# Attention scores in a fused two-block transformer kernel: row halves of 64 instead of 128 contraction rows, issued in pairs

## The reference

```python
# block 0 (per sequence; H = 16 heads, D = 16)
h = _ln(x) * (1 + sc_msa) + sh_msa
qkv = h @ w_qkv + b_qkv                       # one window of 128: plain self attention
scores = einsum('qhd,khd->hqk', q, k) / sqrt(D)
o = einsum('hqk,khd->qhd', softmax(scores), v)
x = x + (o @ w_so + b_so) * g_msa
h = _ln(x) * (1 + sc_mca) + sh_mca            # cross attention to 128 context rows
scores = q k^T / sqrt(D);  keep the 16 largest of each row;  softmax over these
x = x + (o @ w_co + b_co) * g_mca
h = _ln(x) * (1 + sc_mlp) + sh_mlp            # SwiGLU, 1024 wide
x = x + (silu(a) * b @ w_m2 + b_m2) * g_mlp
# block 1: adaptive layer norms of x and the context, plain cross attention, x + (out @ Wp + bp)
```

## Time and profile before

| | us |
|---|---|
| time, median of 2 runs | 1040.71 (1040.1 to 1041.33) |
| span of the profiled execution | 1041.6 |
| PE, busy matmul time | 852.6 |
| DVE | 669.1 |
| ACT | 515.7 |
| POOL | 501.5 |
| mean granted TensorE clock | 0.947 of 2.4 GHz |

### The profile page before, as it was taken

The page is one execution under the profiler, slowest core; times in us unless marked ns, Lnnn a source line. Parts: engine busy times, 40 slices in busy tenths (PEclk is TensorE's granted clock), DMA queues, the critical chain, the costliest instruction groups (busy, mean ns, idle before and its releaser), DMA issues.

```text
span 1041.6 us, 21054 instructions
## 1 busy us (share of the span) xinstructions
PE 852.6 (82%) x5919; PEld 616.2 (59%) x5919; DVE 669.1 (64%) x2576; ACT 515.7 (50%) x2068; POOL 501.5 (48%) x576
## 2 busy tenths in 40 slices
PE   4879677888889966898898968778898996788897
PEld 4556356666556645676664645656665664566664
DVE  2247888844536888874445689885444679887443
ACT  0257334455557543345565744444455763334555
POOL 3246645633335555453433565554433555555334
PEclk9789899999999988999998998999999998899999
DMA  8441000000100100000000000000000000000000
GB/s 268 123 142 30 18 25 13 18 20 16 31 19 18 30 21 17 21 16 19 24 13 22 27 17 25 15 20 22 16 22 26 12 11 11 11 6 7 1 6 16
DMA packets 33860, 31.15 MB, mean 30 GB/s; under 512 B 7613, under 2 KB 29363, under 8 KB 33475
## 3 DMA queue, kind: packets, MB, share of 16 engines
q1 hardware_dynamic: 33731, 29.66, 9.8%
HBM read 21.20 MB, written 2.15 MB: 22 GB/s over the span
## 4 chain that ended last, share of the span: by engine, by line
PE 47%; DVE 32%; issue 9%; ACT 3%; POOL 3%; SPq 3%; DMA 2%; DVEq 1%; POOLq 0%; ACTq 0%
PE dense_bank L897 9%; PE score_bank L939 9%; PE o_bank L957 6%; DVE left L646 6%; DVE left L657 6%; PE dense_bank L904 6%; PE turn_bank L926 5%; DVE top L640 4%; DVE top L652 4%; PE dense_bank L866 3%; PE dense_bank L875 3%; PE dense_bank L878 2%; PE dense_bank L884 2%; DVE ln_stats L677 2%; DVE x_mid L730 2%
## 5 line engine op out<-in xcount | busy, mean ns | idle before, releaser
L573 ACT ACTIVATE probs<-score_bank,neg_max 128x128 f32<-128x128 f32 x768 | 272.0, 371 | 230.6 <-DVEq L650 146.6
L939 PE MATMUL score_bank<-k_blocks,q_t 128*128 128x512 f32 x384 | 211.6, 640 | 11.3 <-issue 6.2
L567 ACT COPY probs_t<-turn_bank 128x512 f32<-128x512 f32 x192 | 112.7, 587 | 152.7 <-PE turn_bank L926 143.9
L957 PEld LDWEIGHTS o_bank<-probs_t,v_pad 128*32 128x32 f32 x1536 | 73.1, 111 | 163.0 <-issue 96.2
L484 POOL TENSOR_TENSOR probs<-probs,row_sum 128x512 f32<-128x512 f32 x128 | 133.0, 1046 | 72.6 <-DVE row_sum L783 72.1
L573 ACT ACTIVATION_READ_ACCUMULATOR probs<-score_bank,neg_max 128x1 f32 x768 | 160.4, 209 | 0.0
L435 POOL TENSOR_SCALAR ln_var<-ln_mv 128x1 f32<-128x1 f32 x80 | 15.2, 190 | 266.6 <-DVE ln_mv L680 264.9
L957 PE MATMUL o_bank<-probs_t,v_pad 128*32 128x128 f32 x1536 | 125.7, 284 | 19.5 <-issue 19.0
L897 PE MATMUL dense_bank<-h_t,w_m 128*128 128x128 f32 x1024 | 126.6, 282 | 14.2 <-DVEq L694 13.0
L897 PEld LDWEIGHTS dense_bank<-h_t,w_m 128*128 128x128 f32 x1024 | 120.0, 195 | 20.0 <-ACT h_t L533 7.0
L492 POOL TENSOR_SCALAR left<-left 128x512 f32<-128x512 f32 x64 | 95.5, 1492 | 69.0 <-DVE left L657 68.3
(11 more groups left out here) (110 smaller groups left out, 1442.5 us busy)
## 6 DMA issues: line engine op xcount, KB each, us to landing
k_blocks<-k_t SPq DMA_DIRECT2D x384, 16.0 KB, 1.8
gates<-gates_dram SPq DMA_DIRECT2D x16, 384.0 KB, 3.5
k_blocks<-in_L_xcond_w_ada SPq DMA_DIRECT2D x3, 768.0 KB, 9.4
x_in<-in_x SPq DMA_DIRECT2D x16, 128.0 KB, 2.1
ctx_in<-in_ctx SPq DMA_DIRECT2D x16, 128.0 KB, 2.4
w_m<-in_L_xcond_w_m SPq DMA_DIRECT2D x1, 2048.0 KB, 12.3
out_y<-x_mid SPq DMA_DIRECT2D x16, 128.0 KB, 1.7
w_m<-in_L_xcond_w_m SPq DMA_DIRECT2D x1, 1024.0 KB, 14.5
```

Of the source, the lines that this page charges most:

```text
L567: nc.scalar.copy(probs_t[:, u % 3].rearrange("p h t -> p (h t)"), turn_bank[u % TURN_BANKS][:]).then_inc(probs_t_ready, 1)
L573: e = nc.scalar.activation(probs[:, t % 4, h], score_bank[t % SCORE_BANKS][:, P * h:P * h + P], ACT.Exp, bias=neg_max[:, t % 4, h:h + 1], ...
L939: nc.tensor.matmul(score_bank[u % SCORE_BANKS][:], q_t[:, r, c], k_blocks[:, r, c, blk:blk + 4].rearrange("p h t -> p (h t)"), start=True, ...
L957: e = nc.tensor.matmul(o_view[lane:lane + 32, c, what], w, probs_t[:, u % 3, 2 * g + odd], start=(odd == 0), stop=(odd == 1))
```

## The change

The block diagonals shrink to four blocks of 128 columns per chunk, in which head h lies in block h % 4: rows 0 to 63 hold heads 0 to 3 of the chunk and rows 64 to 127 heads 4 to 7, in the same columns. A unit's score matmul contracts only its own 64 rows. PE issues scores only at odd steps (even u), then for both units of a chunk, u on rows 0 to 63 and u+1 on rows 64 to 127, to two banks. For that it waits for exp of unit u-2 (before: u-3 for unit u, and u-2 for unit u+1 a step later). Since PE's scores of an odd unit are no longer issued after the transposes of the unit that used `left` before, DVE waits for these transposes itself, at the head of `top_k`. The setup's weights get an own buffer (`arena`) and, for the last block's two, `left`; the zeroing of L506 and L586, which stays where it is, has half as many elements, as has that of L418.

```diff
-        k_blocks = sb("k_blocks", P, RING, CK, HC, P)
+        k_blocks = sb("k_blocks", P, RING, CK, QH, P)
...
-        arena = k_blocks[:, FIRST:].rearrange("p r c h t -> p (r c h t)")
+        arena = sb("arena", P, CK * NADA + 6 * C)
+        left_flat = left[:].rearrange("p u h t -> p (u h t)")
...
-        ss_q = arena[:, CK * NADA:CK * (NADA + 2 * C)].rearrange("p (c n) -> p c n", c=CK)
-        ss_kv = arena[:, CK * (NADA + 2 * C):CK * (NADA + 4 * C)].rearrange("p (c n) -> p c n", c=CK)
+        ss_q = left_flat[:, 0:CK * 2 * C].rearrange("p (c n) -> p c n", c=CK)
+        ss_kv = left_flat[:, CK * 2 * C:CK * 4 * C].rearrange("p (c n) -> p c n", c=CK)
...
-                    sp.dma_start(k_blocks[rows_h, r, :, h, :], k_t[rows_h, NTH[part] % 3]).then_inc(k_placed[r], 16)
+                    sp.dma_start(k_blocks[rows_h, r, :, h % QH, :], k_t[rows_h, NTH[part] % 3]).then_inc(k_placed[r], 16)
...
-                               zero.broadcast_to([P, CK * HC * P])).then_inc(blocks_zeroed, 1)
+                               zero.broadcast_to([P, CK * QH * P])).then_inc(blocks_zeroed, 1)
...
                 base = (i * 4 * SLOTS + n) * 4
+                dve.wait_ge(turned, i * UNITS + u - 3)
+                dve.sem_inc(dve_passed, 1)
                 for h in range(QH):
...
-                    if 0 <= u < UNITS:
+                    if 0 <= u < UNITS and u % 2 == 0:
 
-                        ph, c, blk = u // 4, u % 4 // 2, 4 * (u % 2)
+                        ph, c = u // 4, u % 4 // 2
...
-                        if u >= SCORE_BANKS:
+                        if u + 1 >= SCORE_BANKS:
 
-                            pe.wait_ge(probs_ready, i * UNITS + u - SCORE_BANKS + 1)
-                        nc.tensor.matmul(score_bank[u % SCORE_BANKS][:], q_t[:, r, c],
-                                         k_blocks[:, r, c, blk:blk + 4].rearrange("p h t -> p (h t)"),
-                                         start=True, stop=True).then_inc(scores_ready, 1)
+                            pe.wait_ge(probs_ready, i * UNITS + u + 1 - SCORE_BANKS + 1)
+                        for half in range(2):
+                            rows_u = slice(64 * half, 64 * half + 64)
+                            nc.tensor.matmul(score_bank[(u + half) % SCORE_BANKS][:], q_t[rows_u, r, c],
+                                             k_blocks[rows_u, r, c].rearrange("p h t -> p (h t)"),
+                                             start=True, stop=True).then_inc(scores_ready, 1)
```

More of the change, by code:

```diff
@@ L215, in block_kernel @@
         FIRST = 2
-        arena = k_blocks[:, FIRST:].rearrange("p r c h t -> p (r c h t)")
         NADA = 9 * C
+        arena = sb("arena", P, CK * NADA + 6 * C)
+        left_flat = left[:].rearrange("p u h t -> p (u h t)")
         w_ada = arena[:, 0:CK * NADA].rearrange("p (c n) -> p c n", c=CK)
-        ss_q = arena[:, CK * NADA:CK * (NADA + 2 * C)].rearrange("p (c n) -> p c n", c=CK)
-        ss_kv = arena[:, CK * (NADA + 2 * C):CK * (NADA + 4 * C)].rearrange("p (c n) -> p c n", c=CK)
-        spare = arena[0:B, CK * (NADA + 4 * C):]
+        ss_q = left_flat[:, 0:CK * 2 * C].rearrange("p (c n) -> p c n", c=CK)
+        ss_kv = left_flat[:, CK * 2 * C:CK * 4 * C].rearrange("p (c n) -> p c n", c=CK)
+        spare = arena[0:B, CK * NADA:]
         gate_bias = spare[:, 0:3 * C]
```

## The result

The changed kernel took **1061.9 us** (1059.89 to 1063.91, two runs) against 1040.71: a ratio of 1.0205, 95% interval 1.0157 to 1.0254. It is slower, by 21 us (whether by more than 2% the interval leaves open); 1018 was forecast, and the time lies outside the range of 1003 to 1045. The profiled execution has a span of 1058.1 us, 16.5 more than before.

A forecast was written before the change was run, and what follows sets the result against it. PE was taken to set the pace in SELF, DVE in CROSS, and PE to be busiest in LAST. Terms -16.5 + 1.5 - 10.7 + 4.2 - 1.2 = -22.7 us took 1040.71 to 1018 us, range 1003 to 1045.

The forecast's parts named there:

- The price of a pair: PE's time for two units' scores: 0.98 us instead of 1.72, with 0.12 for one more tile-shape switch.
- Full overlap: Score matmuls on the two row halves run side by side on PE, streaming 0.86 us for the pair.
- x: PE's cost of a pair of scores, taken as 0.98 us; total time moves by 52 us for each us.
- One-pass overlap: Rival: PE starts passes in order, so only two run together; pair costs 1.41 us, total 1040 us; chance 0.13.
- No overlap: Rival: row halves run one after the other on PE; pair costs 1.84 us, total 1063 us; chance 0.13.
- SELF: Stage where PE sets the pace: 1.03 us net won per four steps, -16.5 us; round starts add +1.5 us.
- at the start of a round: Second and third pairs now wait for exp: 0.5 us for each of three rounds, +1.5 us.
- LAST: Stage with PE busy 80.1 of 90.5 us: shorter scores win 2.67 us a round, -10.7 us over four.
- nothing is won by the shorter PE work: Steps of LAST whose scores stand in front of another wait: no gain, and a pair's second unit costs nothing.
- CROSS: Stage where DVE's top 16 sets the pace: DVE's added wait and two PE steps cost +4.2 us over four rounds.
- Setup: Before the first exp: ACT zeroes half as much, so the first exp starts at about 47.5, -1.2 us.
- The clock: More PE waits could grant more time at 1.2 GHz: up to +8 us, not counted; no chance of its own.

The follow-up runs named there:

- e3: Kernel before with 64-row scores, unit by unit as before, without pairing or DVE's added wait: 1087.32 us, 1.0437.
- e12: Changed kernel with twelve whole-row filler matmuls a round, the pair issued behind o_bank's matmuls and DVE's wait in odd units only: 1028.75 us, 0.9875.
- e5: Changed kernel with ten whole-row filler matmuls a round, results overwritten, only where PE waits long: 1037.87 us, 0.9971.
- e13: Kernel before with one tiny matmul of 64 rows and 4 columns ahead of each unit's whole-row scores: 1089.25 us, 1.0479.
- e4: Kernel before with only DVE's added wait and semaphore increment at the head of top_k: 1048.16 us, 1.0052.

## Why the prediction was wrong, step by step

**The price of a pair: the mechanism right, one term small.** Full overlap was the forecast, and it came. But the change of the array's layout was put at 0.12 us by o_bank's 0.10, and a pair costs 0.20: from the transposes to the scores 0.53 us instead of 0.43, from the scores to o_bank 1.06 instead of 0.96 (e3 shows the same, and here the step at t mod 4 = 3 went from 2.67 to 2.87 us). The switch itself was well judged, 0.09 to 0.10. The other 0.10 lies between the first and the second passes, where the sum had nothing; what causes it was not tried. At 52 us per us of x the 0.08 are 4 us. The steps without a wait are where they were put: 3.01 us forecast and 3.01 measured at t mod 4 = 2, 2.96 and 2.97 at t mod 4 = 0.

**The rivals.** One-pass overlap rested on the rule of the Trainium skill ("TensorE: Matmul & The Clock Gate", Part 3, What overlaps and what doesn't) that matmuls start strictly in order. The starts 6 ns apart, ahead of the first half's second pass, contradict it for row halves. No overlap was forecast to give 1063 us, and 1061.9 was measured; it is false nevertheless, since the passes' busy time fell by half. Whoever had looked at the time alone would have taken it for shown.

**SELF: -16.5 + 1.5 forecast, +0.9 measured.** The four steps at 2.4 GHz gained 0.74 us instead of 1.03 (the 0.08 above in both pairs, and a wait for exp that costs 0.55 us instead of 0.45: the step at t mod 4 = 1 went from 1.96 to 2.71 us, where 2.08 + 0.45 = 2.53 was put). The failing step is "at the start of a round ... 0.5 us for each of three rounds": the pair's new wait for exp leaves PE idle for 2.4 us there, and what follows runs at 1.2 GHz. The step t = 3 grew from 5.20 to 7.63 us, 5.7 of it at 1.2 GHz (means of four rounds). With that filled and the pair behind the values (e12), SELF takes 186.7 us in four rounds, 7.6 less than before; 15 less was forecast.

**LAST: -10.7 forecast, +10.9 measured.** Of the steps that were counted some came: -0.46 us at t = 40 (-0.45 forecast), -0.85 at t = 44 (-0.86 forecast), +0.20 at t = 35 and 39 (+0.12 each). But t = 42 and 43 together gained 0.28 us where they run at 2.4 GHz (0.74 was forecast), and the 0.86 us that t = 46 gained came back whole at t = 47 in the first three rounds. PE in that step, before and after:

```profile
791.25 1.16 PE L875 MATMUL dense_bank<-h_t,w_qkv 128*128 128x128 f32 x8
```
```profile
800.15 1.16 PE L878 MATMUL dense_bank<-h_t,w_qkv 128*128 128x128 f32 x8 [0.84 <-ACT h_t L534]
```

The scores of t = 46 were on the chain, but ACT's copy, exps and eviction of h_t ran beside them and end as late as before: with shorter scores PE waits 0.84 us for them. Shortening a piece of the chain wins only the lead that it has over the work beside it. The two steps' missing gains make some 5 us in four rounds. e5 bears this out: with its clock back, LAST is 4.4 us shorter than before, not 10.7.

What failed most is the sentence that in steps with a wait behind the scores "nothing is won by the shorter PE work". It is worse: shorter scores make the wait longer, and PE comes out of it at 1.2 GHz. The steps t = 36 and 38, forecast unchanged, took 8.93 and 9.41 us instead of 7.71 and 7.58 (means of four rounds). With fillers, the filler's 0.86 us at the step's head included, they take 7.71 and 7.29.

**CROSS: +4.2 forecast, +7.5 measured.** DVE's wait costs 4.8 instead of 3.2; the lower clock there (109 us at 1.2 GHz) is mostly hidden behind top_k. What makes up the other 1.7 us was not tried.

**Setup: -1.2 forecast, -2.8 measured.** The first exp starts at 45.94 instead of 48.73. ACT's zeroing:

```profile
43.58 1.99 ACT L587 COPY k_blocks<-one_cols 128x1024 f32<-128x1024 f32 x2 [14.66 <-DVE glu L800]
```

It is 1.70 shorter than in the earlier trace rows, and exp no longer waits for it, as forecast. But it also begins 1.55 us earlier, in the setup's DMA and norms, where executions differ by more than this (43.4 to 48.7 us for the first exp over all kernels here).

**The clock: named, and left out of the sum.** The step that decided is "up to +8 us on it and don't count it in the sum". The part at 1.2 GHz grew by 57 us in SELF and LAST; PE takes twice as long in it where it works, so it is worth at most about 29 us (an estimate from these parts), and the fillers, which cost time themselves, gave 24 back. With the pair's longer start (4 us), the smaller repairs (4.7), two further fillers (4.4) and the gains that LAST never had (5), up to 42 of the 44 us between 1018 and 1061.9 have a name; that these parts add up is argued, not measured, and they may overlap. The clock was weighed as a matter of waits alone. It has two causes in this change, the pair's longer waits (whole rows in pairs: 0.924 to 0.940) and the half rows (without pairs: 0.899 to 0.904), and the second was not thought of.

## What to carry to other kernels

Before PE is given less to do, look at what it does between its waits: where the granted clock is kept up by work, work removed near a wait can come back as 1.2 GHz on the dense matmuls behind it, and the stage gets longer. Put that in the sum as a term of its own: the dense matmuls behind each wait that grows, at double their time. A few useless whole-row matmuls inside such waits, each tried in its place, can be worth more than the change itself (1061.9 to 1037.9 us here), while in a kernel that has its clock they cost a few us (1045.8 instead of 1040.7). And a piece of the chain that gets shorter gives back only the time until the next engine's work ends: count what runs beside it (t = 46 and 47 in LAST).

## What the hardware showed that was not expected

- Two matmuls of 64 rows on different halves of the array, whose outputs go to different banks, start 6 ns apart, and the second one's first pass starts 0.53 us before the first one's second pass, against their order in the program. A pair of 2 x 2 passes of 512 columns takes 1.06 us to the next matmul.
- Matmuls of 64 rows hold the clock less than matmuls of 128 rows that stream for as long: 0.88 (e3) against 0.97 (e13) in SELF of round 2, with PE busy nearly all the time in both. As fillers they return next to nothing in LAST (0.94 in round 2), where whole-row ones bring 0.93 to 1.00.
- Scores of 64 rows instead of 128 between matmuls of 128 rows cost 0.20 us more: 0.10 ahead of the first pass, and 0.10 between the first and the second one, which start 0.53 us apart instead of 0.43. The same 0.53 stands between the passes of whole-row scores behind a matmul of 64 rows (e13). A two-pass matmul of 4 columns and 64 rows holds PE for 0.31 us there.
- A wait of DVE for a semaphore that had already been reached, with an increment of another behind it, costs 0.07 us each time (e4), in a stage where DVE sets the pace.
